# One block for routing, experts and last norm; constants made during attention, list columns made directly

## The reference

```python
mod = (_silu(L0_c) @ L0_wmod).reshape(L0_c.shape[0], 6, 1, -1)
...
h = _layernorm(x, axis=-1) * (1 + ca) + sa
x = x + ga * _L0_attn_ref(h, L0_attn_Wq, L0_attn_Wkv_down, L0_attn_Wk_up, L0_attn_Wv_up, L0_attn_Wo)
h = _layernorm(x, axis=-1) * (1 + cb) + sb
x = x + gb * _L0_ffn_ref(h, ...)
```

```python
kv, ki = jax.lax.top_k(key_mat, cap)
tok = flat_tok[ki]
gate = jnp.where(valid, w_flat[ki], 0.0)
xe = x[tok]
...
out = jnp.zeros_like(x).at[tok.reshape(-1)].add((y * gate[..., None]).reshape(-1, H))
```

## Time and profile before

| | |
|---|---|
| median of 3 runs | 1398.02 us (1397.46 to 1400.77) |
| the profiled execution | 1400.17 us |
| its span in the profile | 1398.3 us |
| PE, DVE, ACT, POOL busy | 1164.2, 994.2, 754.7, 974.1 us |
| attention | to about 1030 us of the span |
| routing | about 1030 to 1154 us |
| experts | about 1154 to 1318 us |
| last norm | about 1322 to 1398 us |

### The profile page before, as it was taken

How to read it: one execution, slowest core, us unless ns; L and a number is a source line. 1 busy time by engine, 2 the same in 40 slices (tenths; PEclk the granted TensorE clock), 3 DMA queues, 4 the chain that set the end, 5 groups by cost and what they waited for, 6 DMA issues and landing times. The chain is left out here.

```text
span 1398.3 us, 23882 instructions
## 1 busy us (share of the span) xinstructions
PE 1164.2 (83%) x5973; PEld 784.3 (56%) x5974; DVE 994.2 (71%) x2205; ACT 754.7 (54%) x1482; POOL 974.1 (70%) x1092
## 2 busy tenths in 40 slices
PE   7899999999999999999999999999921273979400
PEld 5556666665666656566565656656511263979400
DVE  4887777776777777677777767677358873767397
ACT  4665765666576565657566565755315132444144
POOL 3386878879687887978888796877660165555268
PEclk9999999999999999999999999999955555999755
DMA  4000101011010110101011000101140104232285
GB/s 147 17 18 16 62 1 62 19 43 46 15 60 0 61 37 24 46 15 60 1 61 45 15 32 17 46 2 46 46 128 2 60 0 99 43 94 44 62 267 169
DMA packets 68429, 70.89 MB, mean 51 GB/s; under 512 B 12864, under 2 KB 63984, under 8 KB 68224
## 3 DMA queue, kind: packets, MB, share of 16 engines
q1 hardware_dynamic: 46752, 47.18, 10.6%
q10 hardware_dynamic: 16896, 16.78, 3.6%
q0 software_dynamic: 4704, 6.11, 2.8%
HBM read 40.35 MB, written 29.45 MB: 50 GB/s over the span
## 5 line engine op out<-in xcount | busy, mean ns | idle before, releaser
L556 ACT ACTIVATE PF<-PS 128x512 f32<-128x512 f32 x512 | 298.2, 595 | 256.8 <-PE PS L926 248.2
L818 DVE TENSOR_REDUCE NMAX<-PS 128x1 f32<-128x512 f32 x512 | 342.2, 681 | 88.3 <-PE PS L935 84.7
L469 POOL TENSOR_TENSOR SF<-SF,PF 128x512 f32<-128x512 f32 x252 | 322.1, 1299 | 14.8 <-ACT PF L556 14.7
L1007 PE MATMUL PS<-PF,V 128*64 128x512 f32 x1024 | 248.0, 605 | 0.0
L925 PE MATMUL PS<-Q,K 128*128 128x512 f32 x512 | 222.2, 434 | 3.1 <-ACT PF L556 3.1
L935 PE MATMUL PS<-K,Q 128*128 128x512 f32 x512 | 205.6, 403 | 10.6 <-DVE NMAX L818 10.2
L926 PE MATMUL PS<-Q,K 128*128 128x512 f32 x512 | 201.4, 393 | 0.0
L575 ACT ACTIVATE Q<-PS 64x512 fp32r<-64x512 f32 x256 | 151.5, 592 | 48.3 <-PE PS L94 43.3
L466 POOL TENSOR_TENSOR SF<-PF 128x512 f32<-128x512 f32 x126 | 162.0, 1301 | 19.6 <-ACT PF L556 19.6
L497 POOL TENSOR_TENSOR XL<-XF,XH 128x512 fp32r<-128x512 f32 x63 | 82.6, 1312 | 128.4 <-ACT XH L630 128.3
L925 PEld LDWEIGHTS PS<-Q,K 128*128 128x128 f32 x512 | 96.4, 188 | 120.7 <-ACT PF L556 55.0
(11 more groups left out here) (325 smaller groups left out, 2524.4 us busy)
## 6 DMA issues: line engine op xcount, KB each, us to landing
X<-in_L_attn_x SPq DMA_DIRECT2D x16, 512.0 KB, 3.5
MODB<-mod_rows SPq DMA_DIRECT2D x16, 512.0 KB, 3.7
h_rows<-H ACTq DMA_DIRECT2D x16, 512.0 KB, 3.0
acc_rows<-H ACTq DMA_DIRECT2D x16, 512.0 KB, 4.1
A<-acc_rows SPq DMA_DIRECT2D x16, 512.0 KB, 8.8
out_x<-X SPq DMA_DIRECT2D x16, 512.0 KB, 2.9
W1F<-in_L_ffn_W SPq DMA_DIRECT2D x3, 1024.0 KB
W2F<-in_L_ffn_W SPq DMA_DIRECT2D x3, 1024.0 KB, 6.0
```

Source lines behind the costliest of these rows:

```text
L469: s_sum.done(pool.tensor_tensor(total, total, tile, ALU.add))
L556: s_exp.done(act.activation(PF[:, u % 8, :], st_bank(u), ACT.Exp))
L818: s_mred.done(dve.tensor_reduce(NMAX[:, p % 2, r:r + 1], mx_bank(u), AX.X, ALU.max, negate=True))
L1007: last = pe.matmul(num_bank(p)[odd * R:(odd + 1) * R, :], V1[:, vp, c, :], PF[:, k % 8, :], start=(c == 0), stop=(c == TC - 1))
```

## The change

- Routing's constants (RANK8, IOT, SPARE, TOK1, LEVEL, STEP, MOVE, NEED and new ones for the table) are made by POOL in the attention block at (-1, 20); LOWER and ECOL by DVE in `same_expert`.
- Routing, experts and last norm stand in one block: no meeting of engines between them. The waits that take its place are on IDX (s_idx), on the key table in DRAM, and SP's wait for the last scatter.
- The blocks of each expert are counted from the first matmul over ASG (a Sign of the keys with a sum, on ACT) during digits 0 to 8, by short POOL and ACT steps and three matmuls; INFO is written at digit 8.
- The selection uses ACT's Sign against the threshold (SGN) and one combined rank (RANK) in place of GT and a sum of two masks.
- OE is gone. Each OA column is one tensor_scalar with two operations and two operands per partition, from IOT: POOL makes 7 of 8 in the first six steps and 5 in the others, DVE the rest, ACT none. OB reads the row of numbers from PSUM (iot_ps). Of the two halves of places only the first is made ahead of the loop, the second in pieces in its first six steps (`second`).
- POOL's start of the semaphores, its first row numbers and the first scatter of zeros run before the list loop (`first_scatter`). A block's gather uses row numbers of its own (TOKN) and is issued ahead of `shift`. DVE makes W1L before it takes the gates.
- The last norm's first batch is loaded in four parts, with a semaphore each.

```diff
-        for phase in (route, experts):
+        expert_tiles(m, sem, sb)
+        with nc.Block() as block:
             with ExitStack() as tiles:
-                phase(nc, ap, m, sem, lambda name, shape, dt=F32: sb(name, shape, dt, tiles))
-        with ExitStack() as tiles:
-            last_norm(nc, out, m, sem, lambda name, shape, dt=F32: sb(name, shape, dt, tiles))
+                route(nc, ap, m, sem, lambda name, shape, dt=F32: sb(name, shape, dt, tiles), block)
...
+            def routing_constants():
...
+                link(pool.iota(RANK8[:, :], pattern=[[-1, E]], base=E, channel_multiplier=0, **f32))
+                link(pool.iota(ECOLI, pattern=[[0, 1]], base=0, channel_multiplier=1))
...
+                    if isinstance(b, int) and (b, n) == (-1, 20):
+                        routing_constants()
...
+                mask(dve.scalar_tensor_tensor(out=m["LOWER"][:, :], in0=DIFF, scalar=float(P), in1=m["SAME"][:, :],
+                                              op0=ALU.is_gt, op1=ALU.mult))
+                dve.wait_ge(s_rc, 2)
+                mask(dve.tensor_scalar(ECOLI, ECOLI, E - 1, None, ALU.bitwise_and))
+                mask(dve.tensor_scalar(m["ECOL"][:, :], ECOLI, float(CAP), float(-1 - BIG), ALU.mult, ALU.add))
...
-            with pool.Fori(0, STEPS // 2) as i:
-                for par in range(2):
-                    j = i * 2 + par
-                    pool.wait_ge(s_oe, j + 1)
-                    pool.tensor_tensor(OA[:, par, 0:RPOOL, :], OE[:, par, 0:RPOOL, :],
-                                       tok[:, bass.ds(j * RING, RPOOL)].unsqueeze(2).broadcast_to([P, RPOOL, SLOTC]),
-                                       ALU.mult).then_inc(s_oa, 1)
...
+    def pool_columns(j):
+        return 7 if j < 6 else 5
+    def pool_made(j):
+        return sum(pool_columns(k) for k in range(j))
+    def weighted(eng, j, r):
+        col = j * RING + r
+        return eng.tensor_scalar(OA[:, j % 2, r, :], IOT[:, 0:SLOTC], af[:, col:col + 1], tok[:, col:col + 1], ALU.is_equal, ALU.mult)
...
+        pool.tensor_scalar(TABLE[:, 3 * E + 1:3 * E + 2], BLOCKS[:, :], 1.0, None, ALU.mult).then_inc(s_nbp, 1)
+        first_scatter(pool, m)
+        for j in range(STEPS):
+            if j % (STEPS // 2) == 0:
+                pool.wait_ge(s_dd, 2 + j // (STEPS // 2))
+            pool.wait_ge(s_mm, j + 1)
+            for r in range(pool_columns(j)):
+                weighted(pool, j, r).then_inc(s_oa, 1)
...
+        act.activation(iot_ps, IOT[:, :], ACT.Copy).then_inc(s_iot, 1)
...
+        act.wait_ge(s_ab, 2 * NDIG + 2)
+        act.activation(SGN[:, :], LOW[:, :], ACT.Sign, bias=CAND[:, NDIG % 2, 0:1], scale=-1.0, accum_out=CNT[:, 1:2]).then_inc(s_sgn, 1)
...
+        for j in range(STEPS):
+            pe.wait_ge(s_ob, j + 1)
+            pe.wait_ge(s_oa, pool_made(j + 1))
+            pe.wait_ge(s_oav, RING * (j + 1) - pool_made(j + 1))
...
+        dve.wait_ge(s_pool, POOL_CONSTS)
...
+        dve.wait_ge(s_kt, 1)
+        m["s_h2out"].wait(dve, NB - 1, 1)
...
+            if d == 8:
+                dve.wait_ge(s_nbt, 3)
+                dve.tensor_copy(m["INFO"][:, :], table_ps[0:1, :]).then_inc(s_info, 1)
...
+        thr = CAND[:, NDIG % 2, 0:1]
+        link(dve.tensor_scalar(EQT[:, :], LOW[:, :], thr, None, ALU.is_equal, ALU.add, accum_out=CNT[:, 2:3]))
+        dve.wait_ge(s_sgn, 1)
+        link(dve.tensor_tensor(CNT[:, 3:4], CNT[:, 2:3], CNT[:, 1:2], ALU.add))
+        dve.sem_inc(s_tot, 1)
+        link(dve.tensor_tensor_scan(SCAN[:, :], EQT[:, :], ZT[:, :], 0.0, ALU.add, ALU.add))
+        link(dve.scalar_tensor_tensor(out=RANK[:, :], in0=SGN[:, :], scalar=FAR, in1=SCAN[:, :], op0=ALU.mult, op1=ALU.add))
+        dve.wait_ge(s_sum, NDIG + 1)
+        link(dve.tensor_scalar(CNT[:, 4:5], tot_ps, 0.5, float(CAP - NT // 2), ALU.mult, ALU.add))
+        link(dve.tensor_tensor(CNT[:, 4:5], CNT[:, 4:5], off_ps, ALU.subtract))
+        link(dve.tensor_scalar(SEL[:, :], RANK[:, :], CNT[:, 4:5], None, ALU.is_le, ALU.add, accum_out=CNT[:, 5:6]))
+        dve.sem_inc(s_tot, 1)
+        link(dve.tensor_tensor_scan(SCAN[:, :], SEL[:, :], ZT[:, :], 0.0, ALU.add, ALU.add))
+        dve.wait_ge(s_sum, NDIG + 2)
+        link(dve.tensor_tensor(CNT[:, 6:7], ECOL[:, :], off_ps, ALU.add))
+        link(dve.scalar_tensor_tensor(out=DST[:, :], in0=SCAN[:, :], scalar=CNT[:, 6:7], in1=SEL[:, :],
+                                      op0=ALU.add, op1=ALU.mult))
+        dve.sem_inc(s_tot, 1)
...
+        def second(j):
+            if j == 0:
+                link(dve.tensor_tensor(EQ[:, :, :], by_tok, by_expert(D12[:, 0, :]), ALU.is_equal))
+            elif j == 1:
+                link(dve.scalar_tensor_tensor(out=EQ[:, :, :], in0=EQ[:, :, :], scalar=float(BIG), in1=by_tok,
+                                              op0=ALU.mult, op1=ALU.add))
...
+                to_integers(1)
+            elif j == 4:
+                to_places(1)
+            elif j == 5:
+                to_floats(1)
+        link(dve.tensor_reduce(D12[:, 0, :], by_tok, AX.X, ALU.min))
+        to_integers(0)
+        to_places(0)
+        to_floats(0)
+        dve.wait_ge(s_iot, 1)
+        for j in range(STEPS):
+            dve.wait_ge(s_mm, j + 1)
+            dve.tensor_tensor(OB[:, j % 2, :, :], iot_ps.unsqueeze(1).broadcast_to([P, RING, P]),
+                              bf[:, j * RING:(j + 1) * RING].unsqueeze(2).broadcast_to([P, RING, P]), ALU.is_equal).then_inc(s_ob, 1)
+            for r in range(pool_columns(j), RING):
+                weighted(dve, j, r).then_inc(s_oav, 1)
...
+def first_scatter(pool, m):
+    start(pool, m["xstreams"])
+    s_init = m["s_init"]
...
+    scatter(pool, m)
...
+        def shift(g):
+            s_sc.wait(pool, g, BT - 1)
+            s_tok.done(pool.tensor_tensor(TOKS[:, :], TOKP[:, :], NOUGHT[:, :], ALU.add))
...
+        def block(e, a, g, k):
+            s_t.wait(pool, g, -1)
+            s_gate.wait(pool, g, -1)
+            s_tok.wait(pool, g, -1)
+            gate(0)
+            s_tok.done(pool.tensor_copy(TOKN[:, :], IDX[:, bass.ds(e * (CAP // P) + k * BT, BT)]))
+            s_tok.wait(pool, g, 0)
+            gate(1)
+            for t in range(BT):
+                off = bass.IndirectOffsetOnAxis(ap=TOKN[:, t:t + 1], axis=0)
+                pool.indirect_dma_start(out=XG[:, t, :], out_offset=None, in_=m["h2_dram"], in_offset=off).then_inc(s_gx.sem, 16)
+            shift(g)
+            s_y.wait(pool, g, -BT - 1)
+            gate(4)
+            scatter(pool, m)
+        pool.wait_ge(m["s_tab"], 16 * TC)
+        m["s_h2out"].wait(pool, NB - 1, 1)
+        pool.wait_ge(m["s_idx"], 1)
+        each(pool, None, block, block)
...
+        for late in range(2):
+            g = total + late
+            s_tok.wait(pool, g, -1)
+            s_tok.done(gate(5))
+            s_tok.wait(pool, g, 0)
+            shift(g)
+            s_y.wait(pool, g, -BT - 1)
+            gate(3)
+            scatter(pool, m)
...
+        def expert(e, a, g):
+            s_w1h.wait(dve, a, 0)
+            s_w1l.done(dve.tensor_tensor(W1L[:, :, :], W1F[:, :, :], W1H[:, :, :].bitcast(F32), ALU.subtract))
+            next_gates(e, g)
...
-            def shift(g):
-                s_sc.wait(pool, g, BT - 1)
-                s_tok.wait(pool, g, -1)
-                gate(0)
-                s_tok.done(pool.tensor_copy(TOKS[:, :], TOKP[:, :]))
...
+    def _(sp):
+        total = sp.value_load(m["INFO"][0:1, 3 * E + 1:3 * E + 2], min_val=2, max_val=E * CAP // BLK)
+        m["xs"]["sc"].wait(sp, total + 2, BLK // P - 1)
+        for c in range(TC):
+            sp.dma_start(A[:, c:c + 1, :], acc_rows[:, c:c + 1, :]).then_inc(s_first[c], 16)
+        for b in range(1, NB):
...
+        def stats(c):
+            if c < TC:
+                dve.wait_ge(s_first[c], 16)
```

More of the change, by code:

```diff
@@ L1090, in route @@
+    ZEROS, BEFORE_AT, POOL_CONSTS = 3, 5, 5
+    m["s_tab"] = s_tab
     kt_ps = PS[:, 0, :]
@@ L1404, in experts @@
+def experts(nc, ap, m, sem, sb, block):
     PS, IDENT, IDX, INFO = m["PS"], m["IDENT"], m["IDX"], m["INFO"]
@@ L1683, in last_norm, with _ @@
-def last_norm(nc, out, m, sem, sb):
+    @block.sync
+    def _(sp):
+        w1, w2 = weight_rows(ap)
+        nact = actives(sp)
+        with sp.Fori(0, nact) as a:
+            e = sp.value_load(INFO[0:1, bass.ds(a + 1, 1)], min_val=0, max_val=E - 1)
+            k_row, f_row = sp.snap(e * KC), sp.snap(e * FC)
+            s_w1l.wait(sp, a, 0)
+            s_w1.done(sp.dma_start(W1F[:, :, :], w1[:, bass.ds(k_row, KC), :]))
+            s_w2l.wait(sp, a, 0)
+            s_w2.done(sp.dma_start(W2F[:, :, :], w2[:, bass.ds(f_row, FC), :]))
@@ new lines, in _, with transposes, mm1, mm2 @@
+    @block.tensor
+    def _(pe):
+        def transposes(g):
+            s_gx.wait(pe, g, 0)
+            s_xl.wait(pe, g, -1)
+            for c in range(KC):
+                for t in range(BT):
```

(42 more changed lines are left out.)

1059 lines of the change are left out of this document (478 added, 581 removed).

## The result

The changed kernel took 1389.78 us (median of 4 runs, 1388.1 to 1390.93) against 1399.39 for the kernel before in the same job (4 runs): ratio 0.993, 95% interval 0.9917 to 0.9942, so it is faster by some 9.8 us, clear of the noise though under 1%. The forecast was 1366.4 with a range of 1356 to 1382: the sign was right, the gain a third of the size. The profiled execution has a span of 1389.2 us, 9.1 less than before.

A forecast was written before the change was run, and what follows sets the result against it. Between about 1030 and 1172 us no engine was full; a string of hand-overs, mostly from DVE, bound the kernel. Savings summing to 31.6 us, taken off the median of 1398.02, gave 1366.4, range 1356 to 1382.

The forecast's parts named there:

- start of the digits: BITS follows the key transposes without waiting for POOL's constants, 3.3 us less, and the first DVE instruction 0.2 sooner.
- selection: From the GT pass to the transposes of DST: passes and small steps removed, net 2.75 us saved.
- table and list entries: From the DST transposes to the list loop: 9.95 us becomes 2.8, the table made during the digits; saves 7.2.
- list loop: Without OE, the loop of 43.3 us takes 40.0, POOL making 92 columns; saves 3.3.
- hand-over to the experts: After L, the closing matmul's end: gather at L + 4.7, first expert matmul at L + 10.9; saves 8.7, bounds 4 and 10.
- second block, rest of the experts: TensorE's wait for the second block's gather falls from 5.38 us to 3.6; saves 1.8, bounds 0 and 8.
- hand-over to the last norm: SP itself waits for the last scatter, and POOL issues it 0.3 us sooner; saves 4.6, bounds 4 and 6.5.
- I take 0.37 a column: List loop: one 128x80 POOL column costs 0.37 us, from MOVE's 0.418 less some 0.05 of overlap.
- slow columns: Rival in the list loop: POOL columns cost 0.56 us each, loop 14.5 us worse, kernel 1381; chance 0.17.
- the bound from LEVEL: List loop: upper bound for a POOL column, LEVEL's 0.419 plus 0.19 for width, 0.61, less overlap 0.56 us.
- hold by DVE's own columns: Rival in the list loop: DVE's 36 columns hold POOL 0.2 us each, +7, kernel 1373.5; chance 0.10.
- a faster clock: Rival: TensorE granted 2.4 GHz in the list loop, -3.0 us, and no second-block stall; kernel 1357; chance 0.15.

The follow-up runs named there:

- e2_forms: Changed kernel plus 32 small POOL instructions on scratch tiles, four of each form, varying operations, operands and width; 1390.11 us in its one run.
- e1_four_columns: Changed kernel with POOL making 4 columns in every step of the list loop and DVE the other 4; 1371.84 us, ratio 0.9818.
- e3_old_loop: Changed kernel with the list loop's old division of labour: DVE makes OE, POOL multiplies five columns at once, ACT three; 1367.78 us, ratio 0.9781.
- e9_before_iota_psum: Kernel before with one edit: OB reads the row of counts from PSUM, where ACT copies it once; 1389.52 us, ratio 0.9937.
- e4_gather_first: Changed kernel with DVE starting W1L only when POOL has issued the gather of the expert's first block; 1386.9 us, ratio 0.9921.
- e6_w1f_waits: Changed kernel with SP loading the second expert's W1F only when the first gather has landed; 1389.76 us, ratio 0.9927.
- e8: Changed kernel with the old list loop, W1L behind the gather's issue, and the last norm's first batch in one load; 1364.81 us, ratio 0.975.
- e10: Kernel of e8 with the register loads of ACT and POOL taken ahead of the wait for IDX; 1362.58 us, ratio 0.9736.

## Why the prediction was right and wrong

| step of the forecast | forecast, us | measured, us |
|---|---|---|
| start of the digits | +3.5 | +3.4 (BITS 4.25 sooner, 0.88 of it from before KEY) |
| moved constants | -0.3 | 0 (not to be told from the spread of attention's end) |
| selection | +2.75 | +2.8 |
| table and list entries | +7.2 | +7.0 |
| list loop | +3.3 | -16.3 |
| hand-over to the experts | +8.7 | +3.05 |
| second block, rest of the experts | +1.8 | +5.4 |
| hand-over to the last norm | +4.6 | +4.7 |
| the last norm itself | 0 | -1.85 |
| sum | 31.6 | 8.2, and 0.9 from before KEY: 9.1 |

**What held.** Four steps came within 0.2 us of the forecast: start of the digits, selection, table and list entries, hand-over to the last norm. They were counted pass by pass and wait by wait from the earlier trace rows.

**The step that failed** is "I take 0.37 a column". It is a term that was mis-sized, and it was mis-sized by its form: MOVE's row has one operation and constants, the new column has two operations and two per-partition operands, and these cost 0.23 more (e2_forms). The forecast had the rival (slow columns, 0.56 each, 1381) and gave it 0.17; even its price was 0.06 short: 92 columns at 0.62 are POOL's whole 57 us. That the bound from LEVEL came near is chance: LEVEL took 0.233 in the changed kernel, so 0.19 of its 0.419 had been waiting, and what the bound lacked were the second operation and the operands, which LEVEL doesn't have. ZTOK (X<-TOK there), without DVE's passes beside it in the changed kernel, took 0.68 for 128 columns, so only 0.23 of its 0.912 had been waiting, not 0.4. The trace of before had no row of the form at all; that is where the range should have gone wider. DVE's columns were mis-sized too, 0.25 (four in 1.01 us in e1_four_columns) for 0.15; beside POOL's that cost nothing in the changed kernel. The estimate from the Trainium skill (GPSIMD Engine Reference, Performance pitfalls for Q7 kernels) of 0.17 us for the two small read commands together agrees with the 2 x 0.08 measured here; taken into the sum it would have brought the forecast near the rival's time.

**A step that the forecast did not have** is OB's operand. It called the hold between OB and POOL's product "some 0.6 us of 1.67"; it was 0.81, and the change removed it by the move of IOT to PSUM (iot_ps), which the forecast never priced. Had the loop kept its division of labour, the same rows give 6.8 us there (36.5 for 43.3), not 3.3, as e3_old_loop and e9_before_iota_psum show. So the change holds two opposite edits in one loop: the operand, worth about 8 us, and the direct columns, which cost 23 us of loop (59.6 for 36.5) and 20.8 in time. The rival of a hold by DVE's own columns did not come true: POOL's took 0.62 us with one or three of them a step, 0.63 to 0.65 with four. Nor did that of a faster clock: it was 0.50 in the loop, and 0.50 also in e3_old_loop, where TensorE idled only 6.5 of 36.5 us.

The rule that the forecast needed stands in the page that it cited for another. The Trainium skill (SBUF — State Buffer, Who interferes with whom) says that a DVE instruction with two SBUF inputs contends with a GpSimd instruction that reads SBUF, and one with at most one SBUF input, outside the 2-port modes, does not. By that rule the traces agree: 1.67 to 1.70 us for the product with OB's inputs both in SBUF, 0.86 with one in PSUM. The same page of the Trainium skill infers that a tensor_tensor leaves GpSimd's making of DMA descriptors alone; here the runs differ, 2.85 us for half a gather beside W1L and 0.97 without it.

**Hand-over to the experts.** The forecast's "gather at L + 4.7, first matmul at L + 10.9" was 0.9 too early at the gather (POOL's loads take 3.3 us, not 2.5). Its own warning, that W1L could hold the gather, came true and cost 1.8; the load of W1F ahead of the rows, which it did not have, cost 2.65 (e4_gather_first, e6_w1f_waits). Before, both came behind the gather's rows, at 1169.12. Timeline of the kernel before:
```profile
1169.36 2.29 DVE L1594 TENSOR_TENSOR W1L<-W1F,W1H 128x2048 fp32r<-128x2048 f32 x1
...
1171.82 0.38 SPq L1477 DMA_DIRECT2D W1F<-in_L_ffn_W  x1
```

**Second block.** The forecast reasoned that the stall would become 3.6 us and forecast the block's transposes at L + 20.7. They came at L + 24.6. The second gather went out at L + 16.7, as forecast (16.4), but from there to the transposes it took 7.93 us and not 4.25: its second half took 2.29 us beside W2L, and the rows came 4.30 behind it, with W2F's load issued before its end. These are the two effects of the first gather again; no run takes them apart here. Since the first block also came later, the stall was 1.19 and the clock stayed at its upper level of 2.4 GHz behind it. So the +5.4 in the table is no success of the forecast: the late first block moved the loss into the row above, and the two rows together measured 8.45 us for 10.5. In the runs, from the end of the first gather's issue to the transposes of the second block it takes 14.2 to 15.0 us in all kernels with this order on POOL (14.8 after; 15.0, 14.25, 14.2, 14.2 and 14.5 in e3, e4, e6, e8 and e10), while TensorE has work for 6 to 7 us behind its first expert matmul. So what is won between gather and first matmul alone is given back in the second block; only an earlier gather moves both. The longer wait costs by the clock too: where rows behind it show 0.50 (e4, e6, e10, waits of 3.74 to 4.24 us) the third block's transposes come 13.4 to 13.6 us behind the second's, and where they show 1.00 (after, e3, e8, waits of 1.19 to 3.16) 11.8 to 12.0.

**The last norm.** Counting the quarter loads as nothing was about 1.2 us wrong: DVE started 2.4 us sooner on the first batch, and the second batch came later. The other 0.6 us of the 1.85 lies within the spread of that distance among kernels with the same code (77.2 to 79.1).

What stays open: why attention ends up to 4 us apart between executions, and how much of the second block's 14.2 us is holds by W1L and W2L (in e10_loads_early POOL's TOKP took 2.30 us beside W1L and a scatter 2.98 beside W2L). No run took these away. Open too: what it is in W1F's load that delays the gather's rows.
